# Graph network kernel: edge preparation and step 0 of the scatter moved ahead of the first pass, scatter gates shifted

## The reference

```python
def sage_conv(x, edge_index, Wl, bl, Wr):        # layer 0, twice with a relu between
    agg = segment_sum(x[src], dst) / maximum(cnt, 1.0)[:, None]
    return agg @ Wl.T + bl + x @ Wr.T

for i in range(HOPS):                            # layer 1, three hops
    Hn = segment_sum(H[src] * edge_weight[:, None], dst) @ Wn[i].T + bn[i]
    H = Hn + H @ Ws[i].T + bs[i]                 # elu but for the last hop

# layer 2: a degree-scaled sum over edges; layer 3: attention with 8 heads over edges
```

## Time and profile before

| | us |
|---|---|
| three runs, median (lowest to highest) | 3041.39 (3030.63 to 3042.83) |
| the profiled execution | 3039.42 |
| its span, first to last instruction | 3037.6 |

### The profile page before, as it was taken

How to read it: one execution, slowest core, us unless ns; L and a number is a source line. 1 busy time by engine, 2 the same in 40 slices (tenths; PEclk the granted TensorE clock), 3 DMA queues, 4 the chain that set the end, 5 groups by cost and what they waited for, 6 DMA issues and landing times. The chain is left out here.

```text
span 3037.6 us, 32378 instructions
## 1 busy us (share of the span) xinstructions
PE 2471.0 (81%) x9483; PEld 1629.1 (54%) x9484; DVE 1394.4 (46%) x3940; ACT 708.7 (23%) x1552; POOL 932.0 (31%) x927
## 2 busy tenths in 40 slices
PE   4777988996884999999999999999947787547680
PEld 2444977434763555565556555677723344435560
DVE  7998755455673001030101001455636555636568
ACT  3777644112442000010001000354400000103112
POOL 0000256665664300000000000012267665566640
PEclk8898998997996999999999999999978989769885
DMA  6656677343332544444444444333287888536541
GB/s 234 246 238 253 198 233 217 126 144 120 111 105 71 167 153 129 156 132 148 135 150 131 149 124 140 103 98 103 77 213 252 266 269 261 188 111 198 179 134 42
DMA packets 209534, 493.89 MB, mean 163 GB/s; under 512 B 46457, under 2 KB 128430, under 8 KB 209134
## 3 DMA queue, kind: packets, MB, share of 16 engines
q1 hardware_dynamic: 134353, 297.50, 30.6%
q10 hardware_dynamic: 39005, 137.07, 13.3%
q0 software_dynamic: 36032, 57.60, 7.1%
HBM read 374.71 MB, written 117.32 MB: 162 GB/s over the span
## 5 line engine op out<-in xcount | busy, mean ns | idle before, releaser
L792 POOL DMA_INDIRECT table_dense_weights<-pair_weight,dst x416 | 408.5, 982 | 607.8 <-DVE weights_c L845 350.6
L1522 PE MATMUL banks<-own_term,features_and_rows 128*128 128x391 f32 (+1 forms) x1656 | 552.3, 491 | 0.0
L2105 POOL DMA_INDIRECT features_and_rows<-table_heads,src x376 | 399.6, 1063 | 223.4 <-issue 105.8
L1522 PEld LDWEIGHTS banks<-own_term,features_and_rows 128*128 128x128 f32 x1656 | 312.2, 189 | 226.8
L1548 DVE TENSOR_SCALAR features_and_rows<-banks,hop_bias 128x391 f32<-128x391 f32 (+1 forms) x24 | 15.0, 624 | 780.2 <-PE banks L1522 780.2
L947 PE MATMUL banks<-split_rows,count_columns 128*128 128x512 f32 x1200 | 320.5, 415 | 17.5 <-issue 9.3
L2506 PE MATMUL banks<-features_and_rows,edge_to_window 128*128 x880 | 232.3, 426 | 107.9 <-DVE edge_to_window L2467 60.0
L1522 PE MATMUL banks<-features_and_rows 128*128 128x391 f32 (+1 forms) x840 | 282.4, 491 | 0.0
L947 PEld LDWEIGHTS banks<-split_rows,count_columns 128*128 128x128 f32 x1200 | 228.6, 194 | 70.9 <-issue 15.6
L2506 PEld LDWEIGHTS banks<-features_and_rows,edge_to_window 128*128 128x128 f32 x880 | 180.2, 209 | 159.9 <-issue 126.2
L558 PE MATMUL banks<-features_and_rows,pair_and_bias_rows 128*128 128x400 f16 x806 | 185.3, 395 | 85.4 <-DVE features_and_rows L540 41.3
(11 more groups left out here) (425 smaller groups left out, 2985.8 us busy)
## 6 DMA issues: line engine op xcount, KB each, us to landing
hidden<-table_counts SPq DMA_DIRECT2D x305, 160.0 KB
table_dense_weights<-weights_c ACTq DMA_DIRECT2D x26, 1600.0 KB, 5.7
own_term<-table_dense_weights SPq DMA_DIRECT2D x52, 782.0 KB
features_and_rows<-table_rows_by_edge SPq DMA_DIRECT2D x58, 528.0 KB
pair_and_bias_rows<-table_edge_rows ACTq DMA_DIRECT2D x52, 512.0 KB
weights_c<-table_edge_rows ACTq DMA_DIRECT2D x52, 512.0 KB
own_term<-table_dense_weights SPq DMA_DIRECT2D x34, 780.5 KB
table_rows_by_edge<-features_and_rows SPq DMA_DIRECT2D x48, 528.0 KB
```

Source lines behind the costliest of these rows:

```text
L792: e.indirect_dma_start(out=self.table, out_offset=bass.IndirectOffsetOnAxis(ap=self.place[:, t:t + 1], axis=0), in_=self.values[:, t:t + 1 ...
L1522: m = e.matmul(psum[b][:, 0:wide], z_block(block)[:, f * P:(f + 1) * P], streamed[tile % STREAM][:, lo - from_column:lo - from_column + wi ...
L2105: e.indirect_dma_start(out=to[:, k, :], out_offset=None, in_=t_h, in_offset=bass.IndirectOffsetOnAxis(ap=src[:, t:t + 1], axis=0)).then_in ...
```

## The change

`edge_prep` parts 1 to 3 stand in DVE's queue right behind the count build, ahead of the tail loop; part 4 stays at n = 4. The first part now waits for the build's last one-hot and for `m_run`, whose product goes to bank 2 and waits for the build alone. The rows of steps 0 and 1 are requested by SP, ahead of its count loads. The 8 sums of step 0 are dealt out over j = 6 to 14 of the tail loop. `widen_group` of the tail loop stands two tiles later. One step is called at every n from 1 on, so steps 1 to 28 stand in the first pass and 29 to 51 in the layers. The gates: h = 8 to 32 in the first pass (from 40 in steps of 3.5 groups), 33 to 66 in the layers at the same products as 27 to 60 were, 67 to 103 in the second pass (112 + 4 (h - 67), capped at 246: tile 24, group 0), none in the hops.

```diff
--- before.py
+++ after.py
@@ -645,8 +645,8 @@
                 rows_out = pr.dma("sp", s_rows, t_rows[r:r + 1, lo * P:(lo + n) * P].rearrange("o (t p) -> t (o p)", p=P),
                                   at_row[0:n, lo:lo + P], t)
         for b in range(2):
-            m_run = T(lambda e, b=b: e.matmul(psum[6][:, 0:2], members[:, b, :], run_pairs[0:PAIR_ROWS, b, 0:2], start=(b == 0),
-                                              stop=(b == 1)), grouped, t)
+            m_run = T(lambda e, b=b: e.matmul(psum[2][:, 0:2], members[:, b, :], run_pairs[0:PAIR_ROWS, b, 0:2], start=(b == 0),
+                                              stop=(b == 1)), grouped, counts_kept)
 
         small_at = COLS + 6 * EDGE_TILES
         target_row, bounds, target = (pre[:, small_at + lo:small_at + hi] for lo, hi in ((0, TAIL), (TAIL, TAIL + 32), (TAIL + 32, TAIL + 34)))
@@ -656,9 +656,9 @@
         def edge_prep():
 
 
-            t = V(lambda e: e.tensor_copy(base_f, base_i))
+            t = V(lambda e: e.tensor_copy(base_f, base_i), (s_step_hot, BUILD_STEPS))
             V(lambda e: e.tensor_copy(group_f, group_i), c_group)
-            V(lambda e: e.tensor_copy(dst_f, dst[:, :]))
+            V(lambda e: e.tensor_copy(dst_f, dst[:, :]), m_run)
             t = V(lambda e: e.memset(before[:, 0:3], -1.0), t)
             t = V(lambda e: e.tensor_copy(last_f, last_i), t)
             V(lambda e: e.tensor_copy(in_step(before)[:, 1:THIRDS, 0:3],
@@ -820,17 +820,15 @@
                 self.in_memory(e, STEPS - 1)
 
         dense_layers_from = [0]
-        IN_ROWS, IN_LAYERS, IN_SECOND, IN_HOPS = 8, 27, 61, 98
+        IN_ROWS, IN_LAYERS, IN_SECOND = 8, 33, 67
 
         def multiplied_beside(e, half_step):
             if IN_ROWS <= half_step < IN_LAYERS:
-                e.wait_ge(s_a_used, min(57 + 4 * (half_step - IN_ROWS), of_group(Q2, 0) - COUNT_GROUPS))
+                e.wait_ge(s_a_used, min(40 + 7 * (half_step - IN_ROWS) // 2, of_group(Q2, 0) - COUNT_GROUPS))
             elif IN_LAYERS <= half_step < IN_SECOND:
                 e.wait_ge(pr.done["pe"], dense_layers_from[0] + 6 * (half_step - IN_LAYERS) - 4)
-            elif IN_SECOND <= half_step < IN_HOPS:
-                e.wait_ge(s_a_used, min(of_group(Q2, 0) - 8 + 4 * (half_step - IN_SECOND), of_group(Q3, 0) - 2 * COUNT_GROUPS))
-            elif half_step >= IN_HOPS:
-                e.wait_ge(s_z_made, 3 * (half_step - IN_HOPS) + 1)
+            elif half_step >= IN_SECOND:
+                e.wait_ge(s_a_used, min(of_group(Q2, 0) - 14 + 4 * (half_step - IN_SECOND), of_group(Q3, 0) - COUNT_GROUPS))
 
         weights = Scatter("weights", t_dense, place_i, pair_weight)
         row_read, summed = {}, {}
@@ -846,24 +844,27 @@
                         out=unread[t % 3][:, 0:n * P], in0=key_row[b][:, of], scalar=pair_key[:, t:t + 1],
                         in1=values(b, of), op0=ALU.is_equal, op1=ALU.mult,
                         accum_out=pair_weight[:, t:t + 1]), landed, summed.get(t - 3))
+                    yield
             row_read[s] = summed[t]
 
-        def load_pair_rows(s):
+        def load_pair_rows(s, queue="act"):
             b = s % 2
             span = slice(s * UNROLL * P, (s + 1) * UNROLL * P)
-            pr.dma("act", s_pair_row[b], key_row[b], t_rows[0:1, span].broadcast_to([P, UNROLL * P]),
+            pr.dma(queue, s_pair_row[b], key_row[b], t_rows[0:1, span].broadcast_to([P, UNROLL * P]),
                    row_read.get(s - 2), zeroed_dense, zeroed_start, rows_out, counts_kept)
-            return pr.dma("act", s_pair_row[b], weight_row[b], t_rows[1:2, span].broadcast_to([P, UNROLL * P]))
+            return pr.dma(queue, s_pair_row[b], weight_row[b], t_rows[1:2, span].broadcast_to([P, UNROLL * P]))
 
         def pair_steps():
 
 
-            landed = {0: load_pair_rows(0), 1: load_pair_rows(1)}
+            landed = {0: load_pair_rows(0, "sp"), 1: load_pair_rows(1, "sp")}
             yield
             for s in range(STEPS):
                 if 1 <= s < STEPS - 1:
                     landed[s + 1] = load_pair_rows(s + 1)
-                sum_pairs(s, landed[s], lambda b, of: weight_row[b][:, of])
+                for _ in sum_pairs(s, landed[s], lambda b, of: weight_row[b][:, of]):
+                    if s == 0:
+                        yield
 
                 def move(e, s=s, ready=row_read[s]):
                     e.wait_ge(*ready)
@@ -977,6 +978,12 @@
 
         counts_kept = (s_window_kept, KEPT_ALL)
 
+        steps = pair_steps()
+        preparing = edge_prep()
+        for _ in range(3):
+            next(preparing)
+        next(steps)
+
         def first_sp(e):
             for n in range(1, NODE_TILES):
                 load_counts(e, Q1, n)
@@ -1005,8 +1012,6 @@
         for j in range(NODE_TILES + AHEAD):
             if j < NODE_TILES:
                 i = 3 + j % 3
-                if j % COUNT_GROUP == 0:
-                    widen_group(Q1, j // COUNT_GROUP, *written)
                 if j not in x_top:
                     x_top[j] = top_of(j, counts_kept)
                 for k in range(K_IN):
@@ -1017,7 +1022,11 @@
                 low_done[j] = x_split = V(lambda e, j=j: e.tensor_tensor(piece(j, 1), x[:, j, :], piece(j, 0), ALU.subtract),
                                           x_top[j], ones_kept if j == 0 else None)
             if j >= AHEAD:
+                if (j - AHEAD) % COUNT_GROUP == 0:
+                    widen_group(Q1, (j - AHEAD) // COUNT_GROUP, *written)
                 tail_products(j - AHEAD)
+            if 6 <= j < 6 + UNROLL + 1:
+                next(steps)
         multiplied_tail = (s_a_used, of_group(Q1, COUNT_GROUPS - 1))
         tail_split = split(K_FOLD, psum[0][:, 0:DIM], multiplied_tail)
         tail_count = lambda h: split_rows[:, K_FOLD, h * SPLIT + DIM:(h + 1) * SPLIT]
@@ -1025,7 +1034,7 @@
         tail_counted = V(lambda e: e.tensor_tensor(tail_count(1), psum[0][:, DIM:SPLIT], tail_count(0), ALU.subtract), t)
 
         fold_of, fold_to, is_node, fold_tmp = (fold_scale[:, n:n + 1] for n in range(4))
-        V(lambda e: e.tensor_copy(fold_scale[:, 0:2], psum[6][:, 0:2]), m_run)
+        V(lambda e: e.tensor_copy(fold_scale[:, 0:2], psum[2][:, 0:2]), m_run)
         t = V(lambda e: e.tensor_scalar(is_node, part[:, 0:1], float(run_row), None, ALU.is_lt))
         t = V(lambda e: e.tensor_scalar(fold_tmp, fold_of, 0.0, None, ALU.is_equal), pr.last("dve"))
         t = V(lambda e: e.tensor_tensor(fold_to, fold_to, fold_tmp, ALU.subtract), t)
@@ -1045,8 +1054,6 @@
 
         widen(Q1 + 1)
 
-        steps = pair_steps()
-        preparing = edge_prep()
         s_fold1 = pr.sem("first_fold_built")
         FIRST_TURN = psum[3]
 
@@ -1125,12 +1132,9 @@
                   inverted, (s_turn1, n - 1) if n > 1 else rows_out, sem=s_kept1)
             if n > 1:
                 keep_first(n - 1)
-            if n == 1:
-                next(steps)
-            if n <= 4:
+            if n == 4:
                 next(preparing)
-            if n >= 3:
-                next(steps)
+            next(steps)
             if n in (9, 14, 19):
                 next(steps)
             if n == LATE_AT:
```

## The result

| | before, us | changed, us | ratio |
|---|---|---|---|
| 20 executions each, median | 3033.09 (3021.71 to 3047.14) | 3062.46 (3043.48 to 3083.67) | 1.009, interval 1.0073 to 1.0107 |
| the profiled execution | 3039.42 | 3075.03 | |

The changed kernel is 27 us slower by the ratio. The forecast was 3037 with a range of 3011 to 3062, so it missed the sign, and the range by half a microsecond. The profiled execution of the changed kernel lies 12.6 us above its median; its trace is read for places, not for the last microsecond.

What follows compares the result with a forecast made beforehand. TensorE was taken as the fullest engine, held up by scatters that make signals reach other engines late, at some 0.44 us each. Terms +4 + 7 - 2 + 2 - 4 - 10 = -3 gave 3036.4, set as 3037, range 3011 to 3062.

Steps and rivals of the forecast that it cites:

- the 4.4 us at the end of the second pass: End of second pass: VectorE heard of TensorE's finished product only 4.4 us behind the last scatter of an unbroken run.
- Preparation ahead of the tail loop: Ahead of the tail loop: edge preparation parts 1 and 2 delay the first low part to 310.9; +4, bounds +2 and +5.
- the "0" for the later widening: Tail loop: widen_group two tiles later alters only ScalarE's order; 0 us, bounds -1 and +1.
- The "0" for the sums and the three first scatters: Tail loop: 8 sums of 0.5 us between low parts fit VectorE's free time; 0, upper bound +1.
- First pass: First pass: 24 more scatters, priced at 0.28 to 0.44 us each; +7, bounds 0 and +14.
- the run decides: Ends of layers and second pass: GpSimd's unbroken scatter run sets the time; up to +10 and -8 us there.
- Rival C: First pass bound by scatters between groups 40 and 121, 96 x 1.58 us, +14 there; +21 in all, 3060; chance 0.20.
- End of the layers: TensorE's wait for the running sum: fewer pair sums ahead, but a longer scatter run; +2, between -7 and +10.
- Second pass and its end: Second pass: same scatter density, 0; its end: 16 scatters rather than 28 in the last run, -4, bounds 0 and -8.
- z of hop 0: z stage of hop 0: its 24 gated and 4 last scatters leave, 36.0 to 25.5 us; -10, bounds -8 and -11.
- The port rule: Skill text: only VectorE and GpSimd contend for a port, so moving scatters gives or costs nothing at ScalarE and TensorE.
- Rival D: Scatters cost others nothing; hop 0 is slow by clock and DMA share; only the tail's +4 is left, 3043; chance 0.07.

Runs made afterwards that it cites:

- widen_early: The changed kernel with the tail loop's widenings two tiles earlier again, as before the change; 1.0018 of the kernel before, in an undelayed session.
- gates_only: The kernel before with only the changed kernel's gates, preparation and steps as before; 1.0000 of the kernel before, in an undelayed session.
- start40_again: The kernel before with first-pass gates from group 40 instead of 57, still 4 groups apart; 3061.78 us, 1.0066 of the kernel before, delayed session.
- slope4: The changed kernel with first-pass gates at 22 + 4 (h - 8) in place of 40 + 3.5 (h - 8); 1.0024 of the kernel before, undelayed.

## Why the prediction was wrong

**What bounds the kernel.** The reading was right that scatters make waits end late, with the 4.4 us at the end of the second pass as its sharpest case. The undelayed sessions bear it out from the other side: there the stretches with scatters or gathers are shorter by 220 us in all, and the hops' blocks take 1171 us in both.

**Preparation ahead of the tail loop: forecast +4, measured +9 to +12 to the first product of the first pass.** The first low part came at 312.85 rather than 310.9, of which 1.5 us is `m_run`, later in this trace, and the stage behind it took 22.3 us where I had left it as it was. The step that failed here was the "0" for the later widening, with bounds of 1 us: TensorE waits at four of the five groups of counts, four times by 1.2 us. The profile of the changed kernel puts two of these waits down to VectorE, but widen_early, where nothing but the widening is put back, loses all four and 3 us of the stage. The "0" for the sums and the three first scatters held within the 1.2 us that are left (17.6 against 16.4). In undelayed sessions the kernels with the moved preparation are 3 to 12 us slower, the changed kernel 6, and the gates cost nothing: what is lost there is lost here.

**First pass: forecast +7 with bounds 0 and +14, measured +22.7 to +26.5, and +5 to +10 more up to the layers. This is the step that failed.** I took the excess of a stretch, divided it by its scatters (0.45 us each) and multiplied by the 24 more. That mean isn't a price, for two reasons. First, most of the excess isn't the scatters': tiles 8 to 24 take 138.3 us in the trace of before and 122.9 in the undelayed trace of gates_only, so 22 of the 37.5 us stand there without any delay, and the scatters' share is 15.4 us, 0.19 each. The largest such piece is in tile 12, TensorE's wait before it turns edge indices, in before and in gates_only:

```profile
413.57 1.94 PE L733 MATMUL banks<-identity,features_and_rows 128*128 128x128 f32 x8 [5.99 <-issue]
...
411.98 1.94 PE L733 MATMUL banks<-identity,features_and_rows 128*128 128x128 f32 x8 [5.33 <-DVE node_of_tail_row L730]
```

Second, and this is the term that was missing: a long unbroken run has a price of its own. Of the changed kernel's 40.2 us over the undelayed pass 16.3 are the run in tile 12, and 23.9 stand beside the rest, 7.5 more than in before. So +7 came near what all but the run cost, by luck, since its price per scatter was made of waits that are not the scatters'; the run was put at nothing. I listed "the run decides" for the hole of the layers and for the second pass's end and left it out where the gates themselves were changed. The right question was how many scatters the open gates permit when GpSimd comes back from a wait: 30, 26, 18, 14 or 10.

**Rival C** had the sign, the place (groups 40 to 121) and nearly the time (3060 against 3062.5). Its mechanism was another: 96 scatters at 1.58 us each, a limit that would hold evenly. The traces show most tiles at 6.5 us and one that all but stands still.

**End of the layers: forecast +2 with -7 to +10.** Measured -6.8, -2.5 and +6.7 in three traces; with the gates alone +10.5. The bounds held; the middle is undecided, and the signals of the chain weren't followed.

**Second pass and its end.** Forecast 0 and -4; measured +9.1, +8.5 and +1.0 for the pass and -0.9 to -4.3 for its end. The pass alone begins worse (15.0 us for the first two tiles against 8.3 in the first trace), with the rest of the run from the layers' end. **Layers** -2 forecast, -1.5 to -3.2 measured. **z of hop 0**: -10 forecast, -11.1 to -12.4 measured; right, and a gain that only delayed sessions have.

**The port rule.** That ScalarE and TensorE share no port with GpSimd (Trainium skill, SBUF — State Buffer, "Who interferes with whom") agrees with the undelayed sessions, where TensorE was busy for 365 us beside 308 scatters in 392 us. It doesn't cover the delayed ones: TensorE, which by it shares nothing with GpSimd, waits 3.12 us for "issue" before one product. Rival D, the time by that rule, had 3043; undelayed, its +4 is close to the +6 measured.

**What stays open.** What makes a session delayed wasn't found, nor why a long run costs more for each scatter than a short one. The spacing of 3.5 groups was not tried apart from its start in a delayed session: start40_again explains 16 to 20 of the 34 us, and the formula gives the spacing 4 more scatters in the run; much of the remainder is at the ends of pass and layers (21.7 and 30.4 us against 6.9 and 15.2), in a trace that lies 10 us above its median. That the earlier start of the scatters gives back in the changed kernel what the gates alone lose (18 against 30 in the run, 12 x 1.26 = 15 us, and 15 us between the two medians) is argued from the traces; neither the preparation with the old gates nor slope4 met a delayed session. No kernel of the study beat the one before.

## What to carry to other kernels

Where one engine's work delays the waits of others, price a moved gate by the longest run that it permits, not by the number of instructions: count what the open gates permit when the gated engine comes back from its longest other wait, less what it has issued. A gate that opens before the engine gets to it doesn't make it start earlier; it only removes the pause. And a mean taken over a stretch is to be broken into its tiles, and what would stand there anyway taken off, before it is used as a price.

## What the runs showed of the hardware

The same kernel took 2809 to 2814 us in some sessions and 3033 to 3046 in others, 8% apart, with each session at one level. The difference lies only where GpSimd issues indirect DMAs, and just behind. Over all traces, undelayed against delayed: the first pass 171 to 180 against 191.0 to 227.6 us (the kernel with only the gates: 174.6 against 227.6), layers 173 to 174 against 194 to 199, second pass 154 to 157 against 179 to 191, the last layers 734 to 744 against 832 to 847, and the hops' blocks, which have none, 1171 in all. In a delayed session an unbroken run of 30 scatters left VectorE asleep for 38.43 us, TensorE between single products, and GpSimd itself waiting 5.10 us more for a gate long open; in an undelayed one TensorE was busy for 365 of 392 us beside 308 scatters with hardly a pause. The granted clock falls with the standstill (0.58 over tile 14, 1.00 over the same tiles undelayed). Measured in one kind of session alone, the same change of the gates comes out as 0 or as +34 us.
